# State-space and expert block: normalization factor on ScalarE, input projection as one block of silus, delta ahead of C, S5 setup reordered

## The chip, the cores and the metric

The kernel runs on one NeuronCore of one Trainium2 chip. The metric is the device time of one execution in microseconds (us), taken as the median of three runs. The core's engines work beside each other, each through its own queue in the order in which the program lists the instructions: PE (TensorE, matmuls), DVE (VectorE), ACT (ScalarE), POOL (GpSimd) and SP, which here only issues DMAs. They meet through semaphores. SBUF is the on-chip memory and PSUM holds the matmul results.

## What is computed

The input x has 8 sequences of 512 steps and 128 channels. All arithmetic is f32.

```python
x = x + S6(layernorm(x))
x = x + moe(layernorm(x))
x = x + S5(layernorm(x))
x = x + moe(layernorm(x))

# S6, on input v: 256 inner channels, 64 states each
xs, res = split(v @ Wi + bi);  xs = silu(xs)
d_raw, B, C = split(xs @ Wx + bx)
delta = softplus(d_raw @ Wdt + bdt)
h_t = exp(delta_t * A) * h_(t-1) + delta_t * B_t * xs_t      # for each channel and state
y = (C * sum_over_states(h) + xs * Dp) * silu(res)
S6 = gamma * normalized(y @ Wo + bo + v) + beta

# moe: 8 experts, the top 2 of the logits, weights by softmax over the two
moe = sum_e weight_e * (silu(v @ W1_e) * (v @ W2_e)) @ W3_e

# S5: 64 complex diagonal states, a linear recurrence over the 512 steps
```

Softplus is computed as relu(z) + ln(1 + exp(-|z|)). Every layernorm divides by sqrt(variance + 1e-5).

## The kernel before

**Tiling.** The 256 x 64 = 16384 recurrences of one sequence are cut into 128 tiles of 128 rows by 512 steps. One tile is one *slot*. For a slot, ACT writes the decays `da = exp(delta * A)` into PSUM (line 736), POOL multiplies the drives `w` into SBUF, two slots at a time (a duo, line 845), DVE runs one scan instruction (line 1146), and PE adds the states into `ys` four slots at a time (line 569). ACT may be 4 slots ahead of DVE (2 buffers of 2 slots), POOL 3 duos, and DVE may be 4 duos ahead of PE.

**Weaving.** `scan(t)` runs the 128 slots of sequence t.b on each engine. Everything else is woven into these slots by `weave`: a task is a generator that yields the slot behind which its next instructions stand in the queue of that engine. During scan b the task `pre_a` prepares sequence b+1 (first normalization, input projection, delta, B and C), `post` finishes sequence b-1 (output projection, normalizations 1 to 4, first expert layer, S5, first half of the second expert layer), and `late` does the second half of the second expert layer of sequence b-2. Ahead of scan 0 the first `pre_a` runs alone with the two setup tasks, and behind scan 7 the last `post` and `late` run alone, where all tasks go by slot with ties in the order pre, setup, S5 setup. An engine works strictly in its order, so an instruction that waits holds up all that stand behind it, the next scan among them.

**Slots.** `LN_AT` gives the slots of the five normalizations: 64, 7, 16, 77, 97. DVE takes the moments there (`moments`, lines 995 and 998). POOL makes the factor six slots later with four instructions of 128x4 (`rstd`, lines 751 to 757: add eps, power -0.5, times mean, times -1). ACT applies it (line 631). `PE_STEPS` gives slots to matmul groups and to one of three PSUM banks H, G, Y each; a bank is refilled when its reader has drained it. The input projection has four tiles `in0` to `in3` in slots 72, 73, 77, 78; ACT makes tanh(z/2) and z/2 + b/2 of each (lines 648, 649) and DVE multiplies them (line 1013). Then come `stepsB` (81), `C0`, `C1` (83, 85), `dt0`, `dt1` (86, 94). For delta ACT makes abs, relu, then exp and ln of both tiles at once (lines 664 to 671), and DVE adds (line 1018); SP stores delta and its product with xs to HBM and reads them back spread over the partitions (lines 319 to 330).

**Experts.** ACT makes four silus in one block every 11 slots (line 684; ACT slots 3, 13, 31, 42, 53, 64, 108, 119). A change between silu and the exp of the decays is a table load, which the compiler puts in. The routing (`routing`) is a chain of small DVE instructions on 128x32; W3 is halved once on POOL in scan 0 (line 766), since the two weights are made as sums with a tanh.

**S5 setup.** `diagonal_setup` makes the S5 matrices and then a table of cosines and sines of 512 steps by doubling (lines 973 to 984) on DVE, all behind the first `pre_a`.

## Time and profile before

| | us |
|---|---|
| median of 3 runs (lowest, highest) | 1941.29 (1937.05, 1941.82) |
| span of the profiled execution | 1936.6 |
| PE / PE weight loads busy | 1377.6 / 611.6 |
| DVE busy | 1522.2 |
| ACT busy | 1294.2 |
| POOL busy | 1516.6 |

The span runs from the first instruction of the program to the last. The median of the runs is 4.7 us above it. In the rows below a start is counted from the span's begin, and what stands in square brackets is how long the engine sat idle before that row and what the profile names as the end of that wait. A merged row (x3) has the first start and the time from it to the last end.

### The profile page before, as it was taken

How to read it: one execution, taken by the hardware profiler on the slowest of the kernel's cores; microseconds unless marked ns; L12 is line 12 of the kernel's file. 1: busy time of each engine (PE TensorE's matmuls, PEld its weight loads, DVE VectorE, ACT ScalarE, POOL GpSimd, SP SyncE). 2: the span in 40 equal slices, each digit the busy share in tenths (PEclk: the TensorE clock that was granted, in tenths of full speed). 3: DMA queues.
4: the chain of work that ended last, by engine and by line, in shares of the span. 5: the costliest groups of instructions: out<-in, count | busy, mean ns of one | idle time of the engine just before them, and what ended most of it. 6: DMA issues, size and time to landing. Idle time of an engine off the chain costs nothing. (4 is left out here: it accounts for less than half of the span.)

```text
span 1936.6 us, 18983 instructions
## 1 busy us (share of the span) xinstructions
PE 1377.6 (71%) x5928; PEld 611.6 (32%) x5928; DVE 1522.2 (79%) x2109; ACT 1294.2 (67%) x2285; POOL 1516.6 (78%) x888
## 2 busy tenths in 40 slices
PE   3236458777885787768776778668787778668958
PEld 1001113224332343224332343224332343324535
DVE  3979887887888788897888888888878878895222
ACT  4447567677777777677777777777776867665423
POOL 0899899788897798877898798977998888974212
PEclk8557569889897989889898899889898898869969
DMA  3500500031001400031000400032000320000000
GB/s 102 195 0 25 184 1 1 25 109 71 12 1 31 173 12 1 25 109 71 12 1 25 169 11 11 1 103 102 11 1 25 109 71 6 1 6 1 6 1 6
DMA packets 34140, 88.34 MB, mean 46 GB/s; under 512 B 5363, under 2 KB 20598, under 8 KB 25846
## 3 DMA queue, kind: packets, MB, share of 16 engines
q1 hardware_dynamic: 32454, 87.12, 12.7%
q8 instruction: 47, 0.77, 0.2%
q14 instruction: 55, 0.45, 0.1%
q10 hardware_dynamic: 1584, 0.01, 0.0%
HBM read 75.58 MB, written 11.53 MB: 45 GB/s over the span
## 5 line engine op out<-in xcount | busy, mean ns | idle before, releaser
L1146 DVE TENSOR_TENSOR_SCAN h<-da,w 128x512 f32<-128x512 f32 x1024 | 1193.2, 1208 | 225.6 <-ACT da L736 127.5
L845 POOL TENSOR_TENSOR w<-ur,br 128x1024 f32<-128x1024 f32 x512 | 1197.1, 2362 | 158.5 <-DVE h L1146 146.3
L736 ACT ACTIVATE da<-dr,al 128x511 f32<-128x511 f32 x1024 | 683.4, 689 | 236.0 <-DVE h L1146 233.3
L569 PE MATMUL ys<-h,wsum 128*32 128x512 f32 x2048 | 331.8, 726 | 243.2 <-DVE h L1146 215.4
L502 PE MATMUL bankH<-nT,w 128*128 128x512 f32 x512 | 321.3, 713 | 99.8 <-DVE aq L1085 67.9
L789 POOL TENSOR_TENSOR x<-x,yk 128x512 f32<-128x512 f32 x128 | 163.2, 1275 | 193.2 <-ACT yk L697 175.2
L502 PE MATMUL bankG<-nT,w 128*128 128x512 f32 x512 | 292.8, 656 | 25.5 <-DVE aq L1085 25.5
L515 PEld LDWEIGHTS bankY<-w,aq 128*128 128x128 f32 x2048 | 259.2, 200 | 83.7 <-issue 74.1
L515 PE MATMUL bankY<-w,aq 128*128 128x128 f32 x2048 | 265.9, 286 | 9.7 <-DVE aq L1085 5.1
L697 ACT ACTIVATE yk<-bankY,rt 128x128 f32<-128x128 f32 x512 | 156.0, 365 | 132.7 <-PE bankY L515 112.3
L569 PEld LDWEIGHTS ys<-h,wsum 128*32 128x32 f32 x2048 | 43.6, 116 | 446.5 <-DVE h L1146 406.2
L502 PEld LDWEIGHTS bankH<-nT,w 128*128 128x128 f32 x512 | 89.1, 213 | 285.5 <-DVE aq L1085 115.0
L502 PEld LDWEIGHTS bankG<-nT,w 128*128 128x128 f32 x512 | 96.8, 209 | 183.9 <-DVE aq L1085 92.6
L1085 DVE TENSOR_TENSOR aq<-tq,bankH 128x512 f32<-128x512 f32 x64 | 42.8, 669 | 62.0 <-PE bankH L502 62.0
L736 ACT ACT_TABLE_LOAD x62 | 79.5, 1283 | 10.3 <-DMA dr<-d_rows 9.2
L472 PE MATMUL bankG<-xs,wx 128*128 128x512 f32 x64 | 43.7, 819 | 43.1 <-DVE sres L1013 42.3
L684 ACT ACT_TABLE_LOAD x55 | 70.6, 1283 | 1.0
L684 ACT ACTIVATE sq<-bankH 128x512 f32<-128x512 f32 x64 | 38.2, 597 | 46.2 <-PE bankH L502 46.2
L684 ACT ACTIVATE tq<-bankH 128x512 f32<-128x512 f32 x64 | 38.3, 599 | 32.4 <-PE bankH L502 32.1
L631 ACT ACTIVATE nrm<-x,nm,rs 128x128 f32<-128x128 f32 x96 | 39.4, 481 | 29.3 <-POOL nm L757 29.2
L1085 DVE TENSOR_TENSOR aq<-tq,bankG 128x512 f32<-128x512 f32 x64 | 42.6, 666 | 12.5 <-PE bankG L502 12.5
L684 ACT ACTIVATE sq<-bankG 128x512 f32<-128x512 f32 x64 | 38.2, 597 | 20.4 <-PE bankG L502 20.4
(178 smaller groups left out, 1040.4 us busy)
## 6 DMA issues: line engine op xcount, KB each, us to landing
br<-b_rows SPq DMA_DIRECT2D x32, 1024.0 KB, 11.7
dr<-d_rows SPq DMA_DIRECT2D x16, 1024.0 KB, 7.7
ur<-u_rows SPq DMA_DIRECT2D x16, 1024.0 KB, 7.5
d_rows<-vh SPq DMA_DIRECT2D x16, 256.0 KB
u_rows<-th SPq DMA_DIRECT2D x16, 256.0 KB
xnew<-in_L_attn_a_x_dram SPq DMA_DIRECT2D x8, 256.0 KB, 3.0
w<-in_L_ffn_W_dram SPq DMA_DIRECT2D x2, 1024.0 KB, 14.6
x<-in_L_attn_a_x_dram SPq DMA_DIRECT2D x8, 256.0 KB, 9.2
```

The source lines that it names most:

```text
L472: ins = nc.tensor.matmul(p[:, :], lhs(k), xs[:, k, :], start=(k == 0), stop=(k == 1))
L502: is_filled(t, f"{name}{m}_{n}", nc.tensor.matmul(p[:, :], wt[:, n // 2, n % 2 * 128:n % 2 * 128 + 128], nT[:, :], start=True, stop=True))
L515: ins = nc.tensor.matmul(p[:, a * 128:(a + 1) * 128], aq[:, (2 * n + k) % 4, a * 128:(a + 1) * 128], w3[:, n, k, :], start=(k == 0), stop= ...
L569: ins = nc.tensor.matmul(ys[32 * q:32 * q + 32, :], wsum[:, :], h[:, (2 * group + q // 2) % H_RING, q % 2, :], start=(n == 0), stop=(n == ...
L631: A(dst[:, a, :], src[:, a, :], ACT.Identity, bias=nm[:, k, a:a + 1], scale=rs[:, k, a:a + 1]).then_inc(normed[k], 1)
L684: A(zt[j % 4], p[:, :], ACT.Silu).then_inc(drained[BANK[f"h{m}_{j}"]], 1)
L697: ins = A(yk[:, a, :], p[:, a * 128:(a + 1) * 128], ACT.Copy, scale=rt[:, 0, a, e:e + 1])
L736: A(da[duo % D_RING][:, k % 2, 1:L], dr[:, half, q, 1:L], ACT.Exp, scale=nega[:, QUADS * half + q, n:n + 1]).then_inc(decay_ready, 1)
L789: G.tensor_tensor(total[:, :, :], total[:, :, :], yk[:, :, :], ALU.add).then_inc(added, 1)
L845: G.tensor_tensor(w[:, duo % W_RING, :, :], ur[:, half, q:q + 2, :], br[:, n:n + 1, :].to_broadcast([128, 2, L]), ALU.mult).then_inc(produ ...
L1085: drain(f"g{m}_{n}", V.tensor_tensor(aq[:, n % 4, :], zt[n % 4], p[:, :], ALU.mult))
L1146: V.tensor_tensor_scan(h[:, duo % H_RING, k % 2, :], da[duo % D_RING][:, k % 2, :], w[:, duo % W_RING, k % 2, :], 0.0, ALU.mult, ALU.add). ...
```

## The change

- **Normalization.** POOL's `rstd` is gone. ACT makes ln(variance + eps) and exp(-0.5 times it) five slots behind the moments, both 128x4, in a table set that holds exp and ln (`DECAYS`). DVE makes -mean times the factor with one instruction three slots behind the moments, from two SBUF tiles (`bag`, `rs`). ACT applies the factor as before.
- **Input projection.** The four matmuls stand in one slot, ACT runs four silus in a block at ACT slot 75 straight from PSUM to their places, with the silu set loaded ahead and the DECAYS set behind. The tanh, the scaled copy and DVE's product are gone.
- **Delta.** `dt0`, `dt1` come in slots 78 and 79, `C0`, `C1` in 84 and 87. DVE's sums of delta stand three slots behind `dt1`.
- **Routing.** In the scans the weight is 1/(1+exp(gap)), with one DVE instruction more; behind the scans a tanh as before. The halving of W3 on POOL is gone.
- **Setup.** The exps of S5 stand ahead of the silus of the first `pre_a`, the sines behind them; the matrices are made ahead of delta, the cosine table behind delta and ahead of C's flag.
- **Table sets** are named by hand.

```diff
 GATES_AT, RES_AT = 44, 54
 PRE_AT = 70
-SETUP_AT = PRE_AT + 32
+GATES_IN_AT = 2
 SETUP_ROWS_AT = PRE_AT + 9
-MATRICES_AT = SETUP_AT + 6
-SCALE_AT = 52
+SETUP_AT = PRE_AT + 10
+MATRICES_AT = PRE_AT + 12
+TURN_AT = PRE_AT + 18
 LN_AT = [PRE_AT - 6, 7, 16, S5_AT, MOE_AT[2] - 8]
-RSTD_LAG, NORM_LAG = 6, 6
-ROUTE = 14
+RSTD_LAG, SHIFT_LAG, NORM_LAG, RESIDUAL_LAG = 5, 3, 7, 6
+ROUTE, LAST_ROUTE = 15, 14
+DECAYS, GATES = "natural_log_exp_and_others", "silu_and_others"
...
-    (0, "H", "xnT"), (2, "G", "in0"), (3, "H", "in1"), (7, "G", "in2"), (8, "H", "in3"), (11, "G", "stepsB"),
-    (13, "G", "C0"), (15, "H", "C1"), (16, "G", "dt0"), (24, "H", "dt1"))]
+    (0, "H", "xnT"), (GATES_IN_AT, "G", "in0"), (GATES_IN_AT, "H", "in1"), (GATES_IN_AT, "G", "in2"), (GATES_IN_AT, "H", "in3"),
+    (6, "G", "stepsB"), (8, "H", "dt0"), (9, "G", "dt1"), (14, "G", "C0"), (17, "G", "C1"))]
...
-                        if n == 0:
-                            pe.wait_ge(outputs_scaled, QUADS)
...
+            act.preload_act_table_set(DECAYS)
 
             def setup():
 
-                yield SETUP_ROWS_AT
+                yield PRE_AT + 1
                 act.wait_ge(loads, 16 * PROJECTION_LOADS)
                 A(al[:, :, :], al[:, :, :], ACT.Exp).then_inc(setup_a, 1)
 
             def diagonal_setup():
-                yield PRE_AT + 1
+                yield PRE_AT + 4
                 act.wait_ge(late_loads, 16 * LATE_LOADS)
                 A(s5w[:, 0:1], s5p[:, 2:3], ACT.Exp).then_inc(diagonal_a, 1)
-                yield SETUP_AT - 2
+                act.wait_ge(rates_ready, 1)
+                A(s5w[:, 3:4], s5w[:, 2:3], ACT.Exp).then_inc(diagonal_a, 1)
+                yield SLOT["in0"] + SILU_LAG
                 act.wait_ge(angles_ready, 1)
-                A(s5w[:, 3:4], s5w[:, 2:3], ACT.Exp).then_inc(diagonal_a, 1)
                 A(s5w[:, 6:7], s5w[:, 4:5], ACT.Sin).then_inc(diagonal_a, 1)
                 A(s5w[:, 7:8], s5w[:, 5:6], ACT.Sin).then_inc(diagonal_a, 1)
-
-            def normalize(k, i, at, src, dst):
-
-                yield at + NORM_LAG + (2 if k == 2 else 0)
-                act.wait_ge(rstd_ready[k], 4 * i + 4)
+                act.preload_act_table_set(DECAYS)
+
+            def normalize(k, i, at, src, dst, reload=False):
+
+                yield at + RSTD_LAG
+                if reload:
+                    act.preload_act_table_set(DECAYS)
+                act.wait_ge(moments_ready[k], 4 * i + 4)
+                A(rs[:, k, :], bag[:, k, :, 1], ACT.Ln, bias=eps[:, 0:1]).then_inc(rstd_ready[k], 1)
+                act.wait_ge(rstd_ready[k], 2 * i + 1)
+                A(rs[:, k, :], rs[:, k, :], ACT.Exp, scale=-0.5).then_inc(rstd_ready[k], 1)
+                yield at + NORM_LAG + (1 if k == 2 else 0)
+                act.wait_ge(shift_ready[k], i + 1)
                 for a in range(TT):
                     A(dst[:, a, :], src[:, a, :], ACT.Identity, bias=nm[:, k, a:a + 1], scale=rs[:, k, a:a + 1]).then_inc(normed[k], 1)
 
@@ -636,31 +651,29 @@
                 yield SLOT["xnT"] + ACT_LAG
                 copy_out(t, "xnT", xnT[:, :])
                 if known(i, 1):
-                    act.wait_ge(halved, 1)
+                    act.wait_ge(first_loads, 16 * FIRST_LOADS)
...
                 for m in range(4):
-                    yield SLOT[f"in{m}"] + ACT_LAG
+                    yield SLOT[f"in{m}"] + SILU_LAG
+                    if m == 0:
+                        act.preload_act_table_set(GATES)
+                        if not known(i, 1):
+                            act.wait_ge(gate_ready, 2 * i)
+                            act.wait_ge(direct_ready, 2 * i)
                     p = got(t, f"in{m}")
-                    if m >= 2:
-                        act.wait_ge(drained[BANK[f"in{m - 2}"]], t.before(f"in{m - 2}") + 1)
-                    elif not known(i, 1):
-                        act.wait_ge(steps_stored[m], 16 * i)
-                        act.wait_ge(inputs_stored[m], 16 * i)
-                    A(th[:, m % 2, :], p[:, :], ACT.Tanh, bias=hbi[:, m:m + 1], scale=0.5).then_inc(tanh_ready, 1)
-                    A(p[:, :], p[:, :], ACT.Identity, bias=hbi[:, m:m + 1], scale=0.5).then_inc(biased_ready, 1)
+                    dst = xs[:, m, :] if m < 2 else sres[:, m - 2, :]
+                    A(dst, p[:, :], ACT.Silu, bias=bis[:, m:m + 1]).then_inc(drained[BANK[f"in{m}"]], 1)
+                if not known(i, 1):
+                    act.preload_act_table_set(DECAYS)
                 yield SLOT["stepsB"] + ACT_LAG
                 if not known(i, 1):
                     act.wait_ge(b_stored, 16 * i)
                 copy_out(t, "stepsB", steps_and_b[:, :], None, ACT.Identity, bias=bxs[:, 0:1])
                 for m in range(2):
-                    yield SLOT[f"C{m}"] + ACT_LAG
-                    if m == 0 and not known(i, 1):
-                        act.wait_ge(gate_ready, 2 * i)
-                    copy_out(t, f"C{m}", cm[:, m, :], None, ACT.Identity, bias=bxc[:, m:m + 1])
-
-                for m in range(2):
                     yield SLOT[f"dt{m}"] + ACT_LAG
                     p = got(t, f"dt{m}")
-                    act.wait_ge(drained[BANK[f"in{m + 2}"]], t.before(f"in{m + 2}") + 1)
+                    if not known(i, 1):
+                        act.wait_ge(steps_stored[m], 16 * i)
+                        act.wait_ge(inputs_stored[m], 16 * i)
                     A(spa[:, m, :], p[:, :], ACT.Abs, bias=bdts[:, m:m + 1]).then_inc(abs_ready, 1)
                     A(p[:, :], p[:, :], ACT.Relu, bias=bdts[:, m:m + 1]).then_inc(relu_ready, 1)
...
                     if name == "h":
+                        if j % 4 == 0 and t.scans:
+                            act.preload_act_table_set(GATES)
                         p = got(t, f"h{m}_{j}")
                         A(zt[j % 4], p[:, :], ACT.Silu).then_inc(drained[BANK[f"h{m}_{j}"]], 1)
+                        if j % 4 == 3 and (t.scans or m == 1 and j == 2 * E - 1):
+                            act.preload_act_table_set(DECAYS)
                     elif name == "gap":
                         act.wait_ge(gap_ready, 2 * c + m)
-                        A(rc[:, 2, :], rc[:, 3, :], ACT.Tanh, scale=0.5).then_inc(gap_tanh_ready, 1)
+                        if t.scans:
+                            A(rc[:, 2, :], rc[:, 3, :], ACT.Exp).then_inc(gap_weight_ready, 1)
+                        else:
+                            A(rc[:, 2, :], rc[:, 3, :], ACT.Tanh, scale=0.5).then_inc(gap_weight_ready, 1)
...
-            def rstd(k, i, at):
-                yield at
-                pool.wait_ge(moments_ready[k], 4 * i + 4)
-                G.tensor_tensor(var[:, k, :], bag[:, k, :, 1], eps[:, :], ALU.add).then_inc(rstd_ready[k], 1)
-                pool.wait_ge(rstd_ready[k], 4 * i + 1)
-                G.tensor_tensor(rs[:, k, :], var[:, k, :], mhalf[:, :], ALU.pow).then_inc(rstd_ready[k], 1)
-                pool.wait_ge(rstd_ready[k], 4 * i + 2)
-                G.tensor_tensor(nm[:, k, :], bag[:, k, :, 0], rs[:, k, :], ALU.mult).then_inc(rstd_ready[k], 1)
-                pool.wait_ge(rstd_ready[k], 4 * i + 3)
-                G.tensor_tensor(nm[:, k, :], nm[:, k, :], minus[:, :], ALU.mult).then_inc(rstd_ready[k], 1)
-
-            def scale_outputs():
-
-                for n in range(QUADS):
-                    yield SCALE_AT + 3 * n
-                    if n == 0:
-                        pool.wait_ge(expert_loads, 16 * EXPERT_LOADS)
-                    part = w3[:, 2 * n:2 * n + 2, :, :].rearrange("p e k c -> p (e k c)")
-                    G.tensor_scalar(part, part, 0.5, None, ALU.mult).then_inc(outputs_scaled, 1)
...
             def diagonal_setup():
 
                 S = lambda n: s5w[:, n:n + 1]
-                yield PRE_AT + 2
+                yield PRE_AT + 4
                 v.wait_ge(late_loads, 16 * LATE_LOADS)
                 v.wait_ge(diagonal_a, 1)
                 chain(V.tensor_scalar(S(1), s5p[:, 0:1], -1e-4, None, ALU.min))
                 chain(V.tensor_tensor(S(2), S(1), S(0), ALU.mult))
+                v.sem_inc(rates_ready, 1)
...
+                yield TURN_AT
                 link(V.memset(cosT[:, 0:1], 1.0))
...
+                yield at + SHIFT_LAG
+                v.wait_ge(rstd_ready[k], 2 * i + 2)
+                V.scalar_tensor_tensor(nm[:, k, :], bag[:, k, :, 0], -1.0, rs[:, k, :], ALU.mult, ALU.mult).then_inc(shift_ready[k], 1)
+
             def pre_a(t):
                 i = t.b + 1
                 yield LN_AT[0]
                 v.wait_ge(x_in, 16 * i + 16)
                 yield from moments(0, i, LN_AT[0], xnew)
-                for m in range(4):
-                    yield SLOT[f"in{m}"] + 3
-                    if m == 0 and not known(i, 1):
-                        v.wait_ge(gate_ready, 2 * i)
-                        v.wait_ge(direct_ready, 2 * i)
-                    v.wait_ge(tanh_ready, 4 * i + m + 1)
-                    v.wait_ge(biased_ready, 4 * i + m + 1)
-                    dst = xs[:, m, :] if m < 2 else sres[:, m - 2, :]
-
-                    drain(f"in{m}", V.scalar_tensor_tensor(dst, th[:, m % 2, :], 1.0, banks[BANK[f"in{m}"]][:, :], ALU.add, ALU.mult))
                 for m in range(2):
-                    yield SLOT["dt1"] + 6 + m
+                    yield SLOT["dt1"] + 3 + m
                     v.wait_ge(relu_ready, 2 * i + m + 1)
                     v.wait_ge(log_ready, i + 1)
                     drain(f"dt{m}", V.tensor_tensor(dl[:, m, :], spa[:, m, :], banks[BANK[f"dt{m}"]][:, :], ALU.add))
+                yield SLOT["C1"] + 2
...
-                link(V.tensor_tensor(R(4), R(2), R(1), ALU.subtract))
-                link(V.tensor_tensor(R(5), R(2), R(1), ALU.add))
+                link(V.tensor_tensor(R(5), R(1), R(2), ALU.subtract))
                 yield SLOT[f"lg{m}"] + 5
-                v.wait_ge(gap_tanh_ready, 2 * c + m)
-                link(V.tensor_tensor(R(4), R(4), spread(rc[:, 2, :]), ALU.mult))
-                drain(f"lg{m}", V.tensor_tensor(rt[:, 0, :, :], R(4), R(5), ALU.add))
+                v.wait_ge(gap_weight_ready, 2 * c + m)
+                if t.scans:
+                    link(V.tensor_scalar(rc[:, 2, :], rc[:, 2, :], 1.0, None, ALU.add))
+                    link(V.reciprocal(rc[:, 2, :], rc[:, 2, :]))
+                else:
+                    link(V.tensor_scalar(rc[:, 2, :], rc[:, 2, :], -0.5, 0.5, ALU.mult, ALU.add))
+                link(V.tensor_tensor(R(5), R(5), spread(rc[:, 2, :]), ALU.mult))
+                drain(f"lg{m}", V.tensor_tensor(rt[:, 0, :, :], R(5), R(2), ALU.add))
```

## Rows read from the trace of the kernel before

**Rows 1.** The page's part 1, busy time of each engine over the whole span.
```profile
PE 1377.6 (71%) x5928; PEld 611.6 (32%) x5928; DVE 1522.2 (79%) x2109; ACT 1294.2 (67%) x2285; POOL 1516.6 (78%) x888
```
**Rows 2.** Stretch, us; busy PE, PEld, DVE, ACT, POOL; clock; DMA. One mid-run period.
```profile
1036.13:1258.00 221.87, 168.58 (x748) 75.58 (x740) 186.34 (x249) 163.17 (x288) 188.83 (x111) 0.88 0.13 47
```
**Rows 3.** Groups by line, same period: busy us, mean ns, idle before, releasers.
```profile
L1146 DVE TENSOR_TENSOR_SCAN h<-da,w 128x512 f32<-128x512 f32 x128 | 149.7, 1208 | 30.6 <-ACT da L736 18.3 <-issue 6.2 <-PE ys L569 5.8
...
L1013 DVE SCALAR_TENSOR_TENSOR xs<-th,bankG 128x512 f32<-128x512 f32 x1 | 0.7, 662 | 0.0
...
L736 ACT ACTIVATE da<-dr,al 128x511 f32<-128x511 f32 x129 | 85.8, 689 | 20.8 <-DVE h L1146 20.4
...
L736 ACT ACT_TABLE_LOAD x9 | 11.5, 1283 | 0.2
...
L845 POOL TENSOR_TENSOR w<-ur,br 128x1024 f32<-128x1024 f32 x65 | 152.3, 2364 | 20.0 <-DVE h L1146 20.0
...
L753 POOL TENSOR_TENSOR rs<-var,mhalf 128x4 f32<-128x4 f32 x5 | 5.1, 1017 | 0.4
```
**Rows 4.** Timeline of the start: start us, duration us, engine, line, instruction.
```profile
13.26 0.20 ACT L619 ACTIVATE s5w<-s5p 128x1 f32<-128x1 f32 x1 [1.75 <-DMA rev<-in_c_rev_dram]
...
35.06 0.69 DVE L1018 TENSOR_TENSOR vh<-th,bankG 128x512 f32<-128x512 f32 x1 [11.26 <-ACT th L671]
...
41.88 0.57 SPq L330 DMA_DIRECT2D dr<-d_rows  x1
...
50.56 6.98 POOL L845 TENSOR_TENSOR w<-ur,br 128x1024 f32<-128x1024 f32 x3 [12.16 <-issue]
63.48 48.53 POOL L845 TENSOR_TENSOR w<-ur,br 128x1024 f32<-128x1024 f32 x21 [5.94 <-DVE h L1146]
...
61.06 53.61 DVE L1146 TENSOR_TENSOR_SCAN h<-da,w 128x512 f32<-128x512 f32 x48 [0.22 <-DVE mc L987]
```
**Rows 5.** Timeline of PE and DVE in the S5 setup, the same columns.
```profile
42.39 0.66 PE L447 MATMUL bankY<-ident,nrm 64*128 64x64 f32 x4 [12.44 <-DVEq L965]
...
38.11 0.30 DVE L929 TENSOR_TENSOR s5w<-s5w 128x1 f32<-128x1 f32 x1 [1.77 <-ACT s5w L624]
...
50.58 2.34 DVE L976 SCALAR_TENSOR_TENSOR s5w<-s5w 128x1 f32<-128x1 f32 x1
...
55.27 2.42 DVE L979 SCALAR_TENSOR_TENSOR sinT<-sinT,s5w,tq 128x128 f32<-128x128 f32 x1
```
**Rows 6.** Timeline of POOL in scan 0, one of four halvings of W3.
```profile
123.79 1.50 POOL L766 TENSOR_SCALAR w<-w 128x512 f32<-128x512 f32 x1
```
**Rows 7.** Timeline of ACT and DVE behind one block of silus.
```profile
1168.58 1.28 ACT L736 ACT_TABLE_LOAD   x1
...
1170.65 1.22 DVE L1146 TENSOR_TENSOR_SCAN h<-da,w 128x512 f32<-128x512 f32 x1 [2.07 <-ACT da L736]
```
**Rows 8.** Timeline of DVE and POOL: waits and products at the touched slots, one period.
```profile
1158.75 3.54 DVE L1146 TENSOR_TENSOR_SCAN h<-da,w 128x512 f32<-128x512 f32 x3 [1.20 <-issue]
...
1229.91 2.35 POOL L845 TENSOR_TENSOR w<-ur,br 128x1024 f32<-128x1024 f32 x1
...
1236.38 1.22 DVE L1146 TENSOR_TENSOR_SCAN h<-da,w 128x512 f32<-128x512 f32 x1 [0.83 <-ACT da L736]
...
1248.16 0.87 DVE L995 BATCH_NORM_STATS2 bst<-x 128x6 f32<-128x128 f32 x4 [2.08 <-POOL x L789]
...
1259.22 3.45 DVE L1146 TENSOR_TENSOR_SCAN h<-da,w 128x512 f32<-128x512 f32 x3 [1.90 <-ACT da L736]
...
1286.13 1.22 DVE L1146 TENSOR_TENSOR_SCAN h<-da,w 128x512 f32<-128x512 f32 x1 [0.52 <-ACT da L736]
...
1286.41 2.36 POOL L845 TENSOR_TENSOR w<-ur,br 128x1024 f32<-128x1024 f32 x1
```
**Rows 9.** Timeline of ACT behind the last scan.
```profile
1786.07 0.62 ACT L684 ACTIVATE tq<-bankH 128x512 f32<-128x512 f32 x1
...
1857.53 1.65 ACT L631 ACTIVATE nrm<-x,nm,rs 128x128 f32<-128x128 f32 x4 [4.69 <-POOL nm L757]
```

62 lines of the change are left out of this document (31 added, 31 removed).

## The prediction

> **What bounds the kernel now.** Part 1 of the page comes first: DVE is busy 79% of the span and POOL 78% [rows 1], so neither is full. The windows then show what repeats: from scan 2 on a period takes 221.87 us, in which POOL works 188.83, DVE 186.34 and ACT 163.17 [rows 2]. The groups by line of that period say where the rest goes. DVE's scan instruction has 30.6 us of idle time before it, POOL's product 20.0 behind DVE, ACT's decay 20.8 behind DVE [rows 3]. They hold each other in turn. Taken place by place in the timeline, DVE waits for decays where ACT had a block of silus, for PE's sums, and for POOL's products. (The profile calls some of the last kind "issue"; they end 0.1 us behind a product.) In most slots the next scan starts as the last one ends, so DVE's queue sets the period, and what DVE does or waits for in it counts in full unless one of these waits stands right behind. Ahead of the scans there is a chain of 61 us, behind the last one some 168 us in which PE leads.
>
> **The start and scan 0: -19.1 us.** Before, delta's first sum starts at 35.06; its store and reload over HBM and POOL's product with xs lead to POOL's first drive at 50.56, 15.5 us later. DVE is then still in the cosine table, and the first scan starts at 61.06, POOL's fourth drive at 63.48 [rows 4]. In the new order ACT's exp of S5 still waits for the late loads until 13.26 [rows 4], now ahead of the silus: 13.3, two small exps and DVE's rates between them 0.9, a table load 1.28, so silus from 15.5 and xs complete at 16.8 (18.86+0.69 before, an estimate from the old spacing). stepsB follows near 20.3, delta's matmuls near 23.3, and ACT's ln, without its table load of 1.28, ends near 27.1. But the sum must also wait for DVE's matrices, now ahead of it: their 4.2 us block (38.11 to PE's start at 42.39) [rows 5] begins only after the copy of the bias rows, which PE makes behind dt1, near 24.9. So delta's sum starts near 29.1, **5.95 us earlier**, and POOL's first drive at 44.6, its end at 46.95. The cosine table takes 18.5 us before, of which three instructions lost 6.45 us to POOL (below). Started at 30.4, with some 1.5 us lost to POOL's two products of delta, it ends at 44.0, hidden behind the reload. The first scan starts at 47.0 instead of 61.06. Worth 14.1, but POOL had three drives ready before, and in scan 0 it is POOL that sets the pace: 21 drives in 48.53 us without a gap, 2.31 each [rows 4]. Its fourth drive moves from 63.48 to 44.6+3x2.31=51.55, **-11.9**. The four halvings of W3 at 1.46 (a row says 1.50 with overlap [rows 6]) lie in that stretch: **-5.84**, DVE waits for POOL throughout it. To slot 71 that makes -17.75. From there the input block costs 2.4 (next part), the ln's two table loads and DVE's delta sums in their old place give back 4.2, waits for ln take 2.6, the rest is POOL's pace; my walk through slots 72 to 127 ends scan 0 **19.1 us earlier**. Bounds: -12 if the table collides with the drives as before, -22 if the silu set's sines and the ln wait cost nothing.
>
> **A period, on DVE's clock.** POOL loses 5 factors of 1.017 and fifteen helpers of 0.2, 8.1 us and 1.2 of gaps [rows 3]. That helps only where DVE waits for it.
> (1) *The new DVE instruction.* nm is one instruction on 128x4 with two SBUF operands. In the S5 setup just such instructions met POOL: one on 128x1 at 50.58 took 2.34 us, two more up to 55.27 took 2.40 and 2.42 where their twins take 0.15 to 0.28, and one at 38.11 took 0.30 until POOL's product ended [rows 5]. Each lasted until the running POOL instruction was over. In the scans DVE's large operations all have one PSUM operand, so the trace has no such wait there. nm brings it five times a period, 0 to 2.31 us plus 0.2. I take the rest of the drive that runs at the new place today: behind scan 67 (ends 1230.95) the drive runs until 1232.2, 1.24; behind scan 100 (1287.35) until 1288.77, 1.4 [rows 8]; slot 19 0.3, since its drives come earlier. The Trainium skill's page "SBUF — State Buffer", section "SBUF: two separate sides", says that DVE and GpSimd share a port pair, taken as an exclusive lock for a whole instruction by a DVE operation with two SBUF inputs or in a 2-port mode. These rows agree; by it the new one-input add on 128x4 in the routing would wait as well, which no row shows.
> (2) *Slots 0 to 26, -1.3.* nm at slot 10 falls ahead of DVE's longest wait for ACT (slot 14, part of the 18.3 of [rows 3]) and is covered; ACT's application of normalization 1 moves behind a decay, -0.6. nm at 19 costs 0.5, and the wait of 1.20 at 1158.75 for a drive [rows 8] is gone with two factors.
> (3) *Slots 64 to 71, +0.6:* 0.2+1.24, less the wait of 0.83 [rows 8], which came from ACT waiting for POOL's nm.
> (4) *Input projection and delta, +1.2.* A block of four silus between two table loads (1.28 each) leaves DVE waiting 2.07 [rows 7]; with the block's wait on PE for its third tile I take +2.2. Four DVE products go, 0.6 each beside a reported 0.66 [rows 3]: -2.4. PE no longer waits for `sres`, so the wait of 1.90 at 1259.22 goes: -1.9. The wait of 2.08 for the expert sum shrinks to 1.3: -0.8. Delta's sums now stand here: +1.2. They wait for ACT: after the block it has eight decays of 0.65, two outputs, stepsB, four abs and relu, exp, normalization 3 and ln to do, 13.4 us, against DVE's 10.7: +2.7, which covers nm of slot 80; and 0.2. The table loads stay at 18 a period: two more for the block, two fewer for ln.
> (5) *Slots 97 to 102, -0.1:* nm 0.2+1.4, less 0.52 of waiting at 1286.13 [rows 8], less delta's sums 1.2.
> (6) *Routing, +1.1:* one instruction more in two chains, 0.2 each; waits for POOL 0 to 2.3, I take 0.7 in one.
> Sum +1.5. Five full periods +7.5, scan 1 the same +1.5 (no late work), scan 7 without pre_a +2.8: **+11.8 us**.
> The skill's page "ScalarE: Activation LUTs", section "What ACT_TABLE_LOAD costs", adds a drain of 1.38 to each load; here the next decay starts 0.01 behind a load of 1.28 [rows 7], so the block is priced without it.
>
> **Behind the last scan: 0.** A factor on POOL costs 1.97 from moments to application, as before the row at 1857.53 [rows 9]; the new path some 0.9. Two of them are alone on the path, -2.1. In the first, a DECAYS load, ln and a silu load come between ACT's outputs and the silus at 1786.07 [rows 9], up to +3.0 less 1.1. I take 0, bounds -3 and +3.
>
> **The sum.** -19.1+11.8+0 = -7.3: the span goes from 1936.6 to 1929.3. The median of the runs was 4.7 above it: **1934.0 us**.
>
> **The rivals.** (A) *nm does not wait for POOL*, being only four columns wide. Then the 1.24, 1.4, 0.3 and 0.7 fall away, 3.6 in each of seven scans, nothing at slots 10 and 80, where another wait covers it: 1934-25 = 1909. Against it stand the four rows of 128x1 and 128x128. (B) *Slower: the waits catch whole drives.* A POOL that is freer sits ready and starts a drive the moment a scan ends, which is when nm is issued. Then slots 19, 67 and 100 cost 2.31 each, +2.0, +1.07 and +0.9, with the routing left as it is: +4.0 in seven scans, 1962. It decides once a period costs more than 1.0 beyond my sum. For it speaks that POOL's 20.0 us of waits end with a scan today [rows 3]; against it, that the nearest are one slot off. (C) *The start is not gained*: the cosine table or the matrices hold the first scan, 7 us less: 1941. (D) *The named table sets do not replace the compiler's loads but add to them*: one more of 1.28 in nine blocks, partly hidden, +6 a period: 1975.
>
> **Chances.** My sum 0.45 (own range 1925 to 1945, from the bounds of start and tail), A 0.20, B 0.20, C 0.10, D 0.05. The range 1909 to 1962 takes in A and B. The measurement tells changes above 0.3%, 5.8 us, that is outside 1935.5 to 1947.1. Faster: 0.26 of the sum's 0.45 and A, 0.46. Same: 0.15 and 0.07 of C, 0.22. Slower: B, D, 0.04 and 0.03, 0.32.
>
> **What would show it.** First scan near 47, POOL's fourth drive near 51.5; nm in DVE's groups with a mean far above 0.2 us, 1 to 1.5; waits of DVE behind ACT near 2.2 at slot 76 and before delta's sum; no wait at slot 84; a period near 223.4. A period under 221 with nm at 0.2 shows A, one over 225 with nm at 2 or more shows B. The sum is wrong if delta's sums wait over 3 us, or if a period changes by more than nm and the block explain.

## The result and the profile after

The changed kernel takes **2014.63 us** in the median (2014.31 to 2016.12) against 1941.05 of the kernel before on the same chip (1937.05 to 1941.82): ratio 1.0388, 95% interval [1.0373, 1.0402]. The forecast was 1934.0, range 1909 to 1962. The measured time lies outside on the slow side. The profiled execution spans 2012.5 us, before 1936.6.

Part 1 of the page, against [rows 1]: POOL lost its factors and the four halvings, 164 of its 888 instructions and 67 us of work. PE took 41 us more for the same matmuls.

```profile
PE 1418.7 (70%) x5928; PEld 636.5 (32%) x5928; DVE 1557.4 (77%) x2128; ACT 1301.6 (65%) x2337; POOL 1449.5 (72%) x724
```

The windows, one period in mid-run, columns as in [rows 2] (stretch, busy PE, PEld, DVE, ACT, POOL, granted clock, DMA):

```profile
1144.86:1380.40 235.54, 175.05 (x741) 79.49 (x740) 192.34 (x253) 163.40 (x293) 181.31 (x91) 0.84 0.13 44
```

A period takes 235.54 instead of 221.87, and every engine is busy for a smaller share of it than in [rows 2]. DVE is busy 6.0 us longer, in which the time that its new instructions are held by POOL is counted as busy; the other 7.7 are idle time before its instructions. PE's granted clock is 0.84 in the mean instead of 0.88: by the clock records of the two traces it stands at the lower level for 75.1 us of this period and for 51.2 of the one before.

The start, timeline, to be read with [rows 4]:

```profile
44.72 23.11 POOL L846 TENSOR_TENSOR w<-ur,br 128x1024 f32<-128x1024 f32 x10 [12.32 <-issue]
47.16 19.65 DVE L1143 TENSOR_TENSOR_SCAN h<-da,w 128x512 f32<-128x512 f32 x17 [3.42 <-POOL w L846]
```

The first scan starts at 47.16 instead of 61.06. That part of the change works. Where it is lost again is seen when the starts of the first scan of each batch are subtracted (all lengths in us, last column the time behind the last scan):

```
                 first    scan 0   scan 1   scan 2   scan 3   scan 4   scan 5   scan 6   scan 7   behind
before            61.1    171.1    214.4    222.2    221.5    221.9    221.9    222.0    212.1    168.6
after             47.2    171.3    219.9    235.4    235.5    235.5    235.5    235.3    222.8    174.0
difference       -13.9     +0.2     +5.6    +13.3    +14.0    +13.7    +13.6    +13.3    +10.8     +5.4
```

The same subtraction every four slots inside scan 5 gives the places. Each number is for the four slots up to the one named; the 32 of them sum to +13.64, and most of those under 0.5 are left out: slot 4 -1.2, 12 +0.6, **20 +4.8**, 28 -1.4, **32 and 36 +3.0**, 64 to 72 +0.8, **76 +6.4**, 80 -1.3, 84 and 88 +1.8, 100 -0.6.

*Slots 28 to 36 and the new instructions.* First the groups of DVE over the whole run (busy us, mean ns, idle before), then the timeline of one of these adds:

```profile
L998 DVE SCALAR_TENSOR_TENSOR nm<-bag,rs 128x4 f32<-128x4 f32 x40 | 47.6, 1191 | 9.1 <-ACT rs L642 9.0
...
L1063 DVE TENSOR_SCALAR rc<-rc 128x4 f32<-128x4 f32 x14 | 15.4, 1102 | 0.0
...
L1064 DVE RECIPROCAL rc<-rc 128x4 f32<-128x4 f32 x14 | 2.5, 178 | 0.5
...
L1066 DVE TENSOR_SCALAR rc<-rc 128x4 f32<-128x4 f32 x2 | 0.3, 164 | 0.0
```

```profile
1210.18 2.35 POOL L846 TENSOR_TENSOR w<-ur,br 128x1024 f32<-128x1024 f32 x1 [4.37 <-DVE h L1143]
...
1210.60 1.96 DVE L1063 TENSOR_SCALAR rc<-rc 128x4 f32<-128x4 f32 x1
1212.59 0.18 DVE L1064 RECIPROCAL rc<-rc 128x4 f32<-128x4 f32 x1
```

nm (-mean times the factor, L998) takes 1.19 us in the mean, the add of four columns 1.10; the same kind of add behind the scans, with POOL at rest, takes 0.16. The one at 1210.60 ends as POOL's product of 1210.18 ends. The mean of the adds mixes two places: 1.95 at slot 33 and 0.25 at slot 110.

*Slots 16 to 20.* Timeline of POOL, DVE and PE, with POOL's two products of the normalization (L802, L805) and the sum of the experts' output (L793):

```profile
1176.30 1.27 POOL L793 TENSOR_TENSOR x<-x,yk 128x512 f32<-128x512 f32 x1 [4.12 <-ACT yk L722]
1177.53 1.27 POOL L802 TENSOR_TENSOR nrm<-nrm,bcs 128x512 f32<-128x512 f32 x1
...
1178.88 1.27 POOL L805 TENSOR_TENSOR x<-nrm,x 128x512 f32<-128x512 f32 x1
...
1180.18 0.87 DVE L992 BATCH_NORM_STATS2 bst<-x 128x6 f32<-128x128 f32 x4 [2.71 <-POOL x L805]
...
1184.86 1.93 PE L574 MATMUL ys<-h,wsum 128*32 128x512 f32 x8 [5.13 <-DVE h L1143]
...
1185.30 2.03 DVE L998 SCALAR_TENSOR_TENSOR nm<-bag,rs 128x4 f32<-128x4 f32 x1
```

nrm is ready (ACT ends it at 1173.93), but on POOL the sum of the experts' output stands in front of it and waits 4.12 us for yk, the weighted outputs that ACT takes from PSUM. In the kernel before, nrm*gamma and x1 came ahead of that sum, and DVE's moments waited for nothing. PE, idle for 5.13 us, then works at 1.2 GHz (window 1184 to 1188: granted clock 0.50).

*Slots 74 to 76.* Timeline of ACT, PE and DVE:

```profile
1279.42 0.63 ACT L722 ACTIVATE yk<-bankY,rt 128x128 f32<-128x128 f32 x2 [5.03 <-PE bankY L520]
...
1282.26 1.28 ACT L658 ACT_TABLE_LOAD   x1
...
1284.30 1.12 PE L464 MATMUL bankG<-xnT,wi 128*128 128x512 f32 x2 [1.66 <-ACT xs L664]
...
1287.03 1.28 ACT L666 ACT_TABLE_LOAD   x1
...
1289.05 2.34 DVE L1143 TENSOR_TENSOR_SCAN h<-da,w 128x512 f32<-128x512 f32 x2 [5.54 <-ACT da L761]
```

ACT comes out of a wait of 5.03 us for PE with no decay in hand, and the scan of slot 74 already waits 1.23. ACT then works 6.1 us on the block without making a decay.

### The profile page after: what moved, and what is told of

It reads as the page before. It is cut to its first block and busy times, and to the rows that moved or that the text cites. A ratio compares the mean times of both kernels' runs of the same rounds, so it can differ in the third digit from the quotient of the medians.

```text
span 2012.5 us, 18826 instructions
## 1 busy us (share of the span) xinstructions
PE 1418.7 (70%) x5928; PEld 636.5 (32%) x5928; DVE 1557.4 (77%) x2128; ACT 1301.6 (65%) x2337; POOL 1449.5 (72%) x724
## 5 line engine op out<-in xcount | busy, mean ns | idle before, releaser
L1143 DVE TENSOR_TENSOR_SCAN h<-da,w 128x512 f32<-128x512 f32 x1024 | 1192.0, 1206 | 232.2 <-ACT da L761 144.9
L574 PE MATMUL ys<-h,wsum 128*32 128x512 f32 x2048 | 340.0, 742 | 279.1 <-DVE h L1143 240.3
L509 PE MATMUL bankH<-nT,w 128*128 128x512 f32 x512 | 325.5, 722 | 89.2 <-DVE aq L1082 50.9
L793 POOL TENSOR_TENSOR x<-x,yk 128x512 f32<-128x512 f32 x128 | 163.0, 1273 | 281.2 <-ACT yk L722 263.9
L520 PEld LDWEIGHTS bankY<-w,aq 128*128 128x128 f32 x2048 | 273.0, 210 | 114.5 <-issue 89.3
L520 PE MATMUL bankY<-w,aq 128*128 128x128 f32 x2048 | 281.6, 296 | 30.7 <-DVE aq L1082 17.9
L473 PE MATMUL bankG<-xs,wx 128*128 128x512 f32 x96 | 60.7, 765 | 22.2 <-DVE vh L1009 21.4
L427 PE MATMUL bankY<-ident,nrm 128*128 128x128 f32 x96 | 23.8, 396 | 52.5 <-ACT nrm L646 46.4
L998 DVE SCALAR_TENSOR_TENSOR nm<-bag,rs 128x4 f32<-128x4 f32 x40 | 47.6, 1191 | 9.1 <-ACT rs L642 9.0
```

The costliest lines, as they stand in the source:

```text
L473: ins = nc.tensor.matmul(p[:, :], lhs(k), xs[:, k, :], start=(k == 0), stop=(k == 1))
L509: is_filled(t, f"{name}{m}_{n}", nc.tensor.matmul(p[:, :], wt[:, n // 2, n % 2 * 128:n % 2 * 128 + 128], nT[:, :], start=True, stop=True))
L520: ins = nc.tensor.matmul(p[:, a * 128:(a + 1) * 128], aq[:, (2 * n + k) % 4, a * 128:(a + 1) * 128], w3[:, n, k, :], start=(k == 0), stop= ...
L574: ins = nc.tensor.matmul(ys[32 * q:32 * q + 32, :], wsum[:, :], h[:, (2 * group + q // 2) % H_RING, q % 2, :], start=(n == 0), stop=(n == ...
L793: G.tensor_tensor(total[:, :, :], total[:, :, :], yk[:, :, :], ALU.add).then_inc(added, 1)
L1143: V.tensor_tensor_scan(h[:, duo % H_RING, k % 2, :], da[duo % D_RING][:, k % 2, :], w[:, duo % W_RING, k % 2, :], 0.0, ALU.mult, ALU.add). ...
```

## The experiments

Spans are those of the profiled executions; up to the fillers at the end they stand 0 to 3.3 us under the medians. Gains and losses are differences of spans. Four theories were on the table: DVE held by POOL's products (nm and the add), POOL's order at slot 20, the block of silus, and delta ahead of C; each against the rival that another wait takes its place.

**nm on POOL.**

```diff
-                yield at + SHIFT_LAG
-                v.wait_ge(rstd_ready[k], 2 * i + 2)
-                V.scalar_tensor_tensor(nm[:, k, :], bag[:, k, :, 0], -1.0, rs[:, k, :], ALU.mult, ALU.mult).then_inc(shift_ready[k], 1)
...
+            def shift(k, i, at):
+                yield at + 6
+                pool.wait_ge(rstd_ready[k], 2 * i + 2)
+                G.tensor_tensor(nm[:, k, :], bag[:, k, :, 0], rs[:, k, :], ALU.mult).then_inc(shift_ready[k], 1)
+                pool.wait_ge(shift_ready[k], 2 * i + 1)
+                G.tensor_tensor(nm[:, k, :], nm[:, k, :], minus[:, :], ALU.mult).then_inc(shift_ready[k], 1)
```

> The changed kernel, but the -mean*rstd of a normalization (nm) is made by two 128x4 products on POOL, in POOL's order between drives, as the kernel before had its last two steps; VectorE has no nm instruction. The work is complete. Theory 1 (the 40 nm instructions, 47.6 us, mean 1191 ns inside the scans against 0.16 us behind them, hold VectorE while POOL writes a drive, and the one at slot 68 also starts the late chain y3, state sum and y1_6 at a granted clock of 0.50): 30 to 45 us shorter than the changed kernel, span 1967 to 1982, and the stretch of the trace before slot 72 shows TensorE at 1.00. Theory 2 (the loss is in the block of silus with its table loads and in the wait for x1, nm only takes up time that VectorE would then spend waiting): less than 12 us shorter, span above 2000.

Measured: 1976.65 us, span 1975.7, **36.8 less** than the changed kernel. Theory 1 holds for the price. Its second half does not: the state sum before slot 72 still ran at the lower clock (1.93 us, window 1246 to 1252 at 0.66), and the wait at slot 76 was 5.54 us as in the changed kernel. nm was not what brought the clock down there, nor what made the block's wait. The run takes nm off DVE and puts two small products on POOL, so 36.8 is the net of both.

**The routing's add in PSUM.**

```diff
-                    link(V.tensor_scalar(rc[:, 2, :], rc[:, 2, :], 1.0, None, ALU.add))
-                    link(V.reciprocal(rc[:, 2, :], rc[:, 2, :]))
+                    link(V.tensor_scalar(p[:, 264:264 + TT], rc[:, 2, :], 1.0, None, ALU.add))
+                    link(V.reciprocal(rc[:, 2, :], p[:, 264:264 + TT]))
```

> The changed kernel, but the 1 + exp of the routing is written to PSUM (the bank that holds the logits) and read from there by the reciprocal; nothing else differs. Theory 1 (a 128x4 add with one source in SBUF and its result in SBUF waits for POOL's drive as the one with two sources does: 14 of them take 1102 ns in the mean, the two behind the scans 164 ns): the add falls to about 0.17 us and the span by 8 to 13 us, to 2000 to 2005. Theory 2 (what it frees is spent at the next wait for TensorE or ScalarE, slots 32 to 36 being held by them): the add falls too, the span by less than 3 us. Theory 3 (the add is slow for another reason, as the source written by ScalarE just before): it stays near 1.1 us.

Measured: 2014.99 us, span 2014.1, no gain. The groups of DVE show why:

```profile
L1067 DVE TENSOR_TENSOR rt<-rt,rc 128x32 f32<-128x32 f32 x16 | 12.7, 793 | 0.6
...
L1063 DVE TENSOR_SCALAR bankY<-rc 128x4 f32<-128x4 f32 x14 | 2.2, 157 | 0.0
```

The add fell to 0.16, and the product two instructions later, with both sources and its result in SBUF, rose from 0.19 to 0.79 in the mean (1.57 at slot 33, where POOL's product still runs, and 0.19 elsewhere). Theory 2's verdict, but by a way that no theory named: the wait went to the next instruction of that kind.

**ScalarE's lag back at 6.**

```diff
-RSTD_LAG, SHIFT_LAG, NORM_LAG, RESIDUAL_LAG = 5, 3, 7, 6
+RSTD_LAG, SHIFT_LAG, NORM_LAG, RESIDUAL_LAG = 5, 3, 6, 6
...
-                yield at + NORM_LAG + (1 if k == 2 else 0)
+                yield at + NORM_LAG + (2 if k == 2 else 0)
```

> The changed kernel, but ScalarE normalizes one slot earlier (lag 6 instead of 7 behind a normalization's slot, the residual's own as it was), as the kernel before had it; this also puts POOL's product nrm*gamma one slot earlier, ahead of the sum of the experts' output that waits for yk. Theory 1 (the +4.8 us between slots 16 and 20 of each period comes from POOL's order: the sum that waited 4.12 us for yk stands ahead of nrm*gamma and x1, for which VectorE's moments then waited 2.71 us, and TensorE's clock fell to 0.50 behind it): 2.5 to 5 us less in each of the seven scans that have this stage, span 1978 to 1995. Theory 2 (the four normalizing instructions, 1.63 us, now stand ahead of the table load and decay 14, so that the wait for that decay, 4.97 us, grows by as much as the other shrinks): within 5 us of the changed kernel.

Measured: 1993.82 us, span 1993.8, **18.7 less**, 3.4 a period. The timeline shows POOL's product ahead of the sum, and the moments without a wait:

```profile
1165.70 1.27 POOL L802 TENSOR_TENSOR nrm<-nrm,bcs 128x512 f32<-128x512 f32 x1 [2.51 <-ACT nrm L646]
...
1170.61 1.28 POOL L793 TENSOR_TENSOR x<-x,yk 128x512 f32<-128x512 f32 x1
1170.80 0.85 DVE L992 BATCH_NORM_STATS2 bst<-x 128x6 f32<-128x128 f32 x4
```

**The block of silus alone, on the kernel before.**

```diff
-                    A(th[:, m % 2, :], p[:, :], ACT.Tanh, bias=hbi[:, m:m + 1], scale=0.5).then_inc(tanh_ready, 1)
-                    A(p[:, :], p[:, :], ACT.Identity, bias=hbi[:, m:m + 1], scale=0.5).then_inc(biased_ready, 1)
+                    dst = xs[:, m, :] if m < 2 else sres[:, m - 2, :]
+                    A(dst, p[:, :], ACT.Silu, bias=hbi[:, m:m + 1]).then_inc(drained[BANK[f"in{m}"]], 1)
```

> The kernel before, of which only the input projection is changed: its four tiles go to TensorE in one slot and are finished by four silus on ScalarE in one block between two table loads, and VectorE's four products are gone; the weights' halving, the normalization on POOL and the order of C and delta stay as they were. Theory 1 (the block is a loss of its own: 4 silus 2.75 us and 2 loads 2.56 us stand together on ScalarE with no lead in front of them, so that a scan waits some 5 us, against 2.6 us of products saved on VectorE): 2 to 5 us more in each scan but the last, span 1950 to 1970. Theory 2 (the block is harmless where VectorE isn't late and TensorE's clock isn't down ahead of it, the wait of 5.54 us in the changed kernel being due to yk that came late): 0 to 2.6 us less in each scan, span 1918 to 1937.

Measured: 1955.43 us, ratio 1.0087 [1.0058, 1.0117], span 1952.1, **15.5 more** than the kernel before. This is theory 1, though the cost is uneven: scans 2 to 6 take 3.2, 3.6, 0.5, 3.0 and 3.3 us more. The wait at slot 76 is 5.54 here too, with nothing of nm in the kernel:

```profile
1243.02 1.93 PE L569 MATMUL ys<-h,wsum 128*32 128x512 f32 x8 [2.91 <-DVE y L1019]
...
1258.54 2.34 DVE L1135 TENSOR_TENSOR_SCAN h<-da,w 128x512 f32<-128x512 f32 x2 [5.54 <-ACT da L736]
```

**The same block without table loads** (tanh in place of silu; only this function differs, so the output isn't the reference's).

```diff
-                    A(dst, p[:, :], ACT.Silu, bias=hbi[:, m:m + 1]).then_inc(drained[BANK[f"in{m}"]], 1)
+                    A(dst, p[:, :], ACT.Tanh, bias=hbi[:, m:m + 1]).then_inc(drained[BANK[f"in{m}"]], 1)
```

> The kernel before with the input projection's block as in the run of that name, but its function is tanh in place of silu, so that ScalarE needs no table load on either side of it; the output is not the reference's, the work is otherwise complete. Theory 1 (the 5 to 6 us wait at slot 76 is the two loads, 2.56 us, on top of four activations in a row): the wait at slot 76 shrinks by 2.2 to 2.9 us and the span by 15 to 21 us, to 1931 to 1937, which is the kernel before or a little less. Theory 2 (the wait is for TensorE's second pair of tiles, which has to wait for the first pair's banks, and the loads stand beside it): under 1.3 us less at slot 76, span above 1943.

Measured: 1939.49 us, span 1939.3. The wait is 2.73 in place of 5.54, the span 12.8 less (15 to 21 expected):

```profile
1246.35 2.34 DVE L1135 TENSOR_TENSOR_SCAN h<-da,w 128x512 f32<-128x512 f32 x2 [2.73 <-ACT da L736]
```

2.81 of the wait went with the two loads of 1.28; the rest is the four activations in a row with the wait for PE's second pair among them.

**Block and delta ahead of C, on the kernel before.**

```diff
-    (13, "G", "C0"), (15, "H", "C1"), (16, "G", "dt0"), (24, "H", "dt1"))]
+    (8, "H", "dt0"), (9, "G", "dt1"), (14, "G", "C0"), (17, "G", "C1"))]
...
-                    yield SLOT["dt1"] + 6 + m
+                    yield SLOT["dt1"] + 3 + m
```

> The kernel before with the block of silus and, in addition, delta made ahead of C with the change's slots (steps and B 76, delta 78 and 79, C 84 and 87, the sums at 82 and 83); the normalization and the setup stay as before. To be compared with the run that has the block alone (span 1952.1, start of the scans 60.5). Theory 1 (the order only brings the first scan forward and is free in the period): first scan 3 to 6 us earlier, periods within 0.5 us, span 1945 to 1950. Theory 2 (the delta sums in front of slots 82 to 84 wait for the logarithm, and P1 and P2 with the clock behind them come late, of which the changed kernel shows +1.8 us between slots 80 and 88 where the block alone shows -2.5): 2 to 4 us more in each period, span 1960 to 1975.

Measured: 1983.68 us, span 1982.3, 30.2 above the block alone, more than either theory said. The first scan came later (68.2): DVE works on the old setup's cosine table until 68.0, behind which the scan starts. In the period DVE waits for the logarithm, and C's matmuls behind it run at 1.2 GHz:

```profile
1295.23 1.28 ACT L671 ACT_TABLE_LOAD   x1
...
1297.78 0.69 DVE L1013 TENSOR_TENSOR vh<-th,bankH 128x512 f32<-128x512 f32 x1 [3.68 <-ACT th L671]
...
1300.23 3.78 PE L471 MATMUL bankG<-xs,wx 128*128 128x512 f32 x4 [5.37 <-DVE vh L1013]
```

The load is one that the changed kernel doesn't have, so this run can't price the order there. The two runs with C ahead of delta, below, do.

**Three parts undone at once.** The edits of the runs with nm on POOL and with the lag at 6, and the weight wholly in PSUM:

```diff
-                    link(V.reciprocal(rc[:, 2, :], rc[:, 2, :]))
+                    link(V.reciprocal(p[:, 264:264 + TT], p[:, 264:264 + TT]))
...
-                link(V.tensor_tensor(R(5), R(5), spread(rc[:, 2, :]), ALU.mult))
+                link(V.tensor_tensor(R(5), R(5), spread(p[:, 264:264 + TT]), ALU.mult))
```

> The changed kernel with nm made on POOL and ScalarE's lag at 6, both at once, and the routing's 1 + exp and its reciprocal both in PSUM, from where the product takes them. Theory 1 (the two losses are separate, 36.8 and 18.7 us of span): span 1950 to 1962; the product with the weight stays below 0.25 us, where it took 0.79 us with the weight in SBUF. Theory 2 (both cure the same stretch, slots 16 to 36, of which nm on POOL alone had won 4.9 us a period): span 1963 to 1975.

Measured: 1965.63 us, span 1962.5, between the theories: 50.0 less than the changed kernel, where 36.8 and 18.7 make 55.5. The weight wholly in PSUM was never run alone, so its own share is not shown. With the whole weight in PSUM the product is at 0.19 again, the add at 0.16:

```profile
L1077 DVE TENSOR_TENSOR rt<-rt,bankY 128x32 f32<-128x32 f32 x16 | 3.0, 186 | 0.5
...
L1073 DVE TENSOR_SCALAR bankY<-rc 128x4 f32<-128x4 f32 x14 | 2.2, 156 | 0.0
```

**C ahead of delta**, first on the changed kernel, then on top of those three:

```diff
-    (6, "G", "stepsB"), (8, "H", "dt0"), (9, "G", "dt1"), (14, "G", "C0"), (17, "G", "C1"))]
+    (11, "G", "stepsB"), (13, "G", "C0"), (15, "H", "C1"), (16, "G", "dt0"), (24, "H", "dt1"))]
...
-                    yield SLOT["dt1"] + 3 + m
+                    yield SLOT["dt1"] + 6 + m
```

> The changed kernel, but C is made ahead of delta at the kernel before's slots (steps and B 81, C 83 and 85, delta 86 and 94, its sums at 100 and 101); the cosine table moves behind the sums accordingly. Theory 1 (with delta ahead of C the sums stand in front of slots 82 to 84 and wait for the logarithm, C's first matmuls follow at the clock's lower level, and P1 and P2 come late: a loss of its own, 3 to 4.5 us a period, which the kernel before with the block showed too): the periods are 2.5 to 4.5 us shorter, the first scan 3 to 9 us later, span 1990 to 2003. Theory 2 (that run's loss was the two table loads around the logarithm, 2.56 us, of which the changed kernel has none, since ln and exp are of one set): periods within 0.7 us of the changed kernel's, span 2013 to 2023.

Measured: 2005.57 us, span 2004.5, only 8.0 less and between the two theories. The periods are 232.3, 232.2, 235.3, 232.2, 235.3: three of them a good 3 us shorter, two not at all.

> The run with nm on POOL, the lag at 6 and the routing's weight in PSUM (span 1962.5, periods of 228.7 us), and in addition C ahead of delta at the kernel before's slots. What is left of the change is the logarithm's way to the normalization factor, the block of silus, the new setup's order and the weights without halving. Theory 1 (order costs by itself): periods 2.5 to 4.5 us shorter, span 1938 to 1950. Theory 2 (no cost without table loads): periods within 0.7 us, span 1962 to 1972. By either, the periods stay 2 to 4 us above the kernel before's 221.8, which is the block (3.0 us a period by its own run).

Measured: **1925.49 us, ratio 0.9932 [0.9909, 0.9954], faster than both kernels**; span 1923.7, 38.8 less than with three parts undone, 6.8 a period, more than either theory said. The same edit on the changed kernel alone had given 8.0. The periods are 221.9, so "2 to 4 above the kernel before" was wrong: the wait at slot 76 is there (+6.0 against before at slots 72 to 76), but slots 24 to 36 and 80 to 84 give back 3.0 and 3.2, and the whole period differs by 0.0. What remains of the change is a gain at the start (first scan 50.3) and in scans 0, 1 and 7, less 7.0 us lost behind the last scan.

**The kernel before with the new setup and unhalved weights.**

```diff
-                weave(pair, [gates(t)] + ([scale_outputs()] if known(t.b, 1) else []) + tasks_of(t, pre_a, post, late))
+                weave(pair, [gates(t)] + tasks_of(t, pre_a, post, late))
...
                 v.sem_inc(matrices_ready, 1)
 
+                yield TURN_AT
...
+                link(V.tensor_scalar(p[:, 264:264 + TT], rc[:, 2, :], -0.5, 0.5, ALU.mult, ALU.add))
```

> The kernel before with two things of the change alone: the setup reordered (exponentials of the diagonal early, Sin behind the input projection with its table load behind it, the cosine table behind the delta sums) and W3 not halved, the routing's weight being made by tanh with its linear step in PSUM. The input projection, the normalization on POOL, and C ahead of delta stay as in the kernel before. Theory 1 (these two are the part of the change that gains, and it is kept to the end since nothing in the steady period is touched): first scan 3 to 9 us earlier than 61.1, scan 0 3 to 6 us shorter, the other scans the same within 0.3 us each, span 1921 to 1931, faster than both kernels by at least 0.3%. Theory 2 (the first scan is set by delta's chain and the loads, with C ahead of it, and the halvings are under the scan's own time): within 3 us of 1936.6.

Measured: **1928.52 us, ratio 0.9952 [0.9936, 0.9969]**, span 1926.8; first scan 57.7, scan 0 -3.3, the steady scans 221.8 to 221.9. This is theory 1, and the second kernel that beats both.

**Fillers.** By now the steady scans (2 to 6) had come in five lengths only. Four, eight, two or sixteen unused bn_stats (the instruction that takes a normalization's moments, here on a 128x128 tile) on the kernel before ask what a small cost really costs (in the traces the four take 0.84 us, the eight 1.62, the sixteen 3.17):

```diff
+            def filler(t):
+                yield 92
...
+                for a in range(4):
+                    V.bn_stats(pad[:, a, :], cosT[:, 0:128]).then_inc(padded, 1)
```

> The kernel before with four more BATCH_NORM_STATS of a 128x128 tile on VectorE at slot 92 of each scan (0.85 us for four in a row by the rows; their result is used by nothing), where VectorE has no wait from slot 89 to 99. Theory 1 (the steady scans come only in lengths some 3.4 us apart: over the ten kernels run so far they lie at 221.8 to 222.3, 224.8 to 225.4, 228.5 to 229.1, 231.7 to 232.3 and 235.3 to 235.5, whatever was undone; a small addition is therefore either swallowed or costs a whole step): scans 2 to 6 at 221.9 or at 225.3 each, nothing between; total of the filler over five scans 0 or multiples of 3.4 us. Theory 2 (time adds up as in the sum of the prediction): 222.2 to 222.8 each, 2 to 4 us over the five.

> The same with eight of them at slot 92 (1.7 us for two times four). Theory 1 (lengths in steps): scans 2 to 6 at 221.9 or 225.3 each, more of them at 225.3 than with four. Theory 2 (addition): 223.0 to 223.6 each, 6 to 8.5 us over the five.

> The kernel before with two BATCH_NORM_STATS of a 128x128 tile on VectorE at slot 92 of each scan, about 0.43 us (half of the four that take 0.85). Theory 1 (steps): scans 2 to 6 each at 221.9 or 225.3; as four of them gave 225.3 in all five, I expect 225.3 in at least three of them. Theory 2 (addition up to a bound): 222.0 to 222.4 each.

> The same with eight of them (1.7 us) at slot 50, where VectorE stands ahead of a wait of 2.42 us for POOL's product in every period. Theory 1 (steps, but only for what moves the chain): 221.9 as in the kernel before, within 0.3. Theory 3 (any change of the instruction stream costs a step): 225.3.

> The same with sixteen of them at slot 92, 3.4 us. Theory 1 (steps): 225.3 or 228.7 in each of scans 2 to 6, 1.7 to 3.4 us apart from what the eight gave (225.3), never between. Theory 2 (addition): 224.7 to 225.3, as the eight's 225.3 would then be a cost of 1.7 plus something fixed, 226.9 to 227.1.

Measured, scans 2 to 6 of the profiled executions, and the medians (before: 1938.7 to 1939.3 beside them):

```
before                    222.2  221.5  221.9  221.9  222.0    1938.7
0.43 us at slot 92        224.0  221.9  221.9  221.9  221.9    1958.0
0.85 us at slot 92        224.8  225.6  225.0  225.3  225.3    1953.5
1.7 us at slot 92         225.3  225.2  225.3  225.6  224.9    1959.9
3.4 us at slot 92         225.4  228.5  225.4  225.7  228.2    1972.8
1.7 us at slot 50         221.8  221.9  221.9  222.2  221.5    1938.4
```

0.85 us cost 3.3 a scan, 1.7 cost 3.4, and 3.4 cost 3.5 or 6.5. 1.7 us in front of a wait cost nothing. The smallest filler is the plainest: its eight executions are 1941.6 and 1944.6 for two, 1957.8 to 1960.4 for six. The same program either swallows 0.43 us (the profiled one is of that kind, but for 1.8 us in its scan 2) or takes some 17 us more, about what five steps of 3.4 would make; no such execution was profiled. I had expected the step in three of its five profiled scans; none had it in full.

The traces say where a step comes from in time, though not why. In scan 5 the filler of 0.85 us adds 0.77 at its own place (slots 92 to 96). The rest stands far behind it, at places where DVE waits for others: +1.2 by slot 108, +1.7 by slot 16, +1.1 by slot 64, +1.5 by slot 76, less 2.8 by slots 28 and 32. PE's clock stands at the lower level for 58.0 us of that scan, against 51.2 in the kernel before and 51.2 in the scans that swallowed the filler of 0.43. The granted clock over the whole run is 0.838 and 0.836 in the two shorter executions of that filler and 0.826 to 0.828 in the six longer ones. So a step comes with more time at 1.2 GHz; which of the two brings the other is not shown.

## Why the prediction was wrong

Forecast and measured span lie 83.2 us apart. Of these, 60.4 come from the five steady periods (13.3 to 14.0 each for a forecast of 1.5), 17.3 from scans 0, 1 and 7, and 5.4 from the stretch behind the last scan.

- **Start.** Right: first scan forecast at 47.0, measured 47.16; POOL's fourth drive 51.55, measured 51.6 (44.72 and three of 2.31).
- **Scan 0.** Forecast 5.0 shorter, measured +0.2. Up to slot 64 it was right: 17.7 us gained in all where I had 17.75, the halvings' 5.84 coming out as 5.8 (slots 52 to 64; the run with the setup alone shows the same). Then nm, 3.49 us here, and the block took +3.4 and +5.9 by slots 68 and 76. This nm was held for more than a drive, which the 0 to 2.31 of (1) and of rival B rule out: it began 1.2 us before the end of one product and lasted to the end of the next.
- **(1) nm.** The mechanism was right and rival A is dead: 36 of the 40 nm met a running product of POOL and ended with a product. At slots 67 and 100, 1.34 and 1.42 were measured for 1.44 and 1.6. At slot 19 it was 2.03 for 0.5. The one at slot 80 held DVE 1.42 and was covered, as forecast (see (4)). Without nm on DVE the run gains 36.8 us. The page "SBUF — State Buffer" of the Trainium skill, section "SBUF: two separate sides", was to decide for the add: by its rule it would wait as well. It did, 1.10 us against 0.16. My 0.7 for the routing was too small: the add held DVE 1.95 at slot 33, and slots 28 to 36 took 3.0 more, against 1.1 forecast for all of (6).
- **(2) Slots 0 to 26, forecast -1.3, measured +2.9 to slot 28.** A failed step: one slot more of lag was priced on ACT alone, -0.6. The constant also places POOL's nrm*gamma, which fell behind a sum that waits for yk, 2.71 us of wait for DVE and a PE at 1.2 GHz behind it. I had walked the moved step along one queue and not along POOL's. With the lag back at 6 the wait is gone and the run gains 18.7 us.
- **(3) Slots 64 to 71.** Forecast +0.6, measured +0.8.
- **(4) Block and delta, forecast +1.2, measured +6.9 (slots 72 to 88).** This is the largest miss and the second failed step. The block's wait was taken as 2.2 from [rows 7], where ACT goes into the block with decays in hand: DVE still has 6.7 us of work behind the first table load. At slot 74 DVE has 1.2: the waits were 1.23 and 5.54, 4.6 more than forecast. The nearer row was the block at slot 14 of the same period of the kernel before, part of the 18.3 us behind decays in [rows 3], where ACT's lead is small too (2.8 us):

```profile
1140.51 1.22 DVE L1146 TENSOR_TENSOR_SCAN h<-da,w 128x512 f32<-128x512 f32 x1 [5.29 <-ACT da L736]
```

  The logarithm's wait was right: 1.36 behind nm's 1.42, and 2.72 in the run with nm on POOL, where I had 2.7 that covers nm. But P1 and P2, the S5 products of PE that DVE reads ahead of slot 87, came late. DVE waited 2.72 for them, 0.71 in the kernel before, which the sum had left out; a wait of 0.88 at slot 88 went in return.

```profile
1277.33 0.69 DVE L1019 TENSOR_TENSOR vh<-th,bankH 128x512 f32<-128x512 f32 x1 [2.72 <-ACT th L684]
```

- **(5)** forecast -0.1, measured -0.5.
- **Behind the last scan.** Forecast 0 with bounds -3 and +3, measured +5.4. The bound counted one detour over the table sets; the trace has it twice in the first 43 us (loads at 1856.63, 1858.47, 1870.37 and 1879.99, none of them in the kernel before), +7.8, and the rest gave back 2.4 (the forecast had 2.1 for two factors, and up to 1.9 lost in one detour).
- **The sum itself.** Even with each term right, adding them would not have given the period. The fillers show that 0.85 and 1.7 us cost the same 3.4, and 0.43 either nothing or about as much. The parts undone one by one (8.0, 18.7, 36.8, and nothing for the add) and together (88.8) don't add up. By the fillers the +1.5 of my sum, had it been right, would have been 3.4 or nothing.
- **Rivals.** B came nearest (slower, through nm), but its ground was wrong: in the periods only slot 19 caught most of a drive, and B's 1962 is still 53 us short. C did not occur, nor D: the period has 18 table loads as before.

In short, two steps of the sum failed: (4) took the block's wait from a place with another lead, and (2) left out POOL's queue. What stays open is what makes the steps. Which of the 13.6 us belongs to nm, order or block is also only settled as "undone alone" and "undone together", for the same reason. Not tested is nm left on DVE with one operand in PSUM.

## What to carry to other kernels

When an instruction is moved by a constant, list every engine whose instructions the constant places, and what stands in front of each there. Take the price of a block from a place where the engine goes in with the same lead, not from one that looks alike. And test a loop whose engines wait for each other with a small filler first: if 0.43 us costs 3.4 or nothing, as here, single terms can't be added, and a part is judged only in the company that it will keep.
